# Self attention in a transformer block: another order of the projections between the heads, and x turned in two halves

## The reference, cut to what matters

```python
x_norm = modulate(_ln(x), shift_a, scale_a)
qkv = x_norm @ W_qkv + b_qkv
attn_w = softmax(einsum('bhqd,bhkd->bhqk', q, k) * scale)
attn_out = (attn_w @ v) @ W_proj + b_proj
x = x + gate_a[:, None] * attn_out
q_c = _ln(x) @ W_qc + b_qc
kv_c = _ln(context) @ W_kvc + b_kvc
...                                   # cross attention of q_c with k_c, v_c; x = x + its projection
h = gelu(modulate(_ln(x), shift_m, scale_m) @ W_mlp1 + b_mlp1) @ W_mlp2 + b_mlp2
x = x + gate_m[:, None] * h
```

## Time and profile before

| | us |
|---|---|
| median of three executions | 3124.63 |
| lowest, highest | 3118.6, 3124.9 |
| the profiled execution, its own time | 3114.64 |
| its span, first to last instruction | 3112.3 |
| TensorE busy in the span | 2748.2 (88%) |
| VectorE busy | 1821.6 (59%) |
| GpSimd busy | 1281.2 (41%) |
| ScalarE busy | 1091.0 (35%) |
| mean granted TensorE clock, share of full | 0.94 |

### The profile page before, as it was taken

How to read it: one execution, slowest core, us unless ns; L and a number is a source line. 1 busy time by engine, 2 the same in 40 slices (tenths; PEclk the granted TensorE clock), 3 DMA queues, 4 the chain that set the end, 5 groups by cost and what they waited for, 6 DMA issues and landing times. The chain is left out here.

```text
span 3112.3 us, 49898 instructions
## 1 busy us (share of the span) xinstructions
PE 2748.2 (88%) x18560; PEld 2183.8 (70%) x18560; DVE 1821.6 (59%) x3386; ACT 1091.0 (35%) x2083; POOL 1281.2 (41%) x1446
## 2 busy tenths in 40 slices
PE   3789989998972699999999999999955999999998
PEld 1667777777752577777777777777634888888886
DVE  2466766766653377777777777776635444444441
ACT  2234434433331144444444444444433211222110
POOL 1234333433330056666666666666761022202211
PEclk9889999999975999999999999999966999999999
DMA  5343434342412233333333333333413111111110
GB/s 167 84 114 82 125 82 126 83 126 79 123 57 88 73 97 105 104 104 104 104 104 104 104 104 104 104 106 83 105 59 112 34 38 48 45 35 39 46 45 21
DMA packets 170390, 269.79 MB, mean 87 GB/s; under 512 B 28967, under 2 KB 85287, under 8 KB 170135
## 3 DMA queue, kind: packets, MB, share of 16 engines
q1 hardware_dynamic: 167079, 259.26, 30.8%
q0 software_dynamic: 3072, 7.34, 0.7%
HBM read 111.04 MB, written 36.77 MB: 47 GB/s over the span
## 5 line engine op out<-in xcount | busy, mean ns | idle before, releaser
L1370 ACT ACTIVATE cross_prT<-cross_tr_ps 125x448 f32<-125x448 f32 x768 | 404.8, 543 | 359.8 <-PE cross_tr_ps L1168 347.6
L1268 DVE TENSOR_REDUCE cross_nmax<-cross_sc_ps 112x1 f32<-112x750 f32 x512 | 459.4, 929 | 37.6 <-PE cross_sc_ps L1151 37.2
L1415 POOL TENSOR_TENSOR cross_part<-cross_prT 125x448 f32<-125x448 f32 x256 | 293.2, 1145 | 339.9 <-PE cross_or_ps L1188 226.1
L860 POOL TENSOR_TENSOR self_psum<-self_prT 112x224 f32<-112x224 f32 x256 | 170.7, 667 | 471.5 <-PE self_or_ps L534 221.7
L1168 PE MATMUL cross_tr_ps<-cross_qst,cross_kst 98*125 98x224 f32 x1536 | 308.8, 286 | 26.8 <-DVE cross_cT_l L1251 22.3
L1168 PEld LDWEIGHTS cross_tr_ps<-cross_qst,cross_kst 98*125 98x125 f32 x1536 | 242.1, 188 | 101.6 <-issue 45.3
L1151 PE MATMUL cross_sc_ps<-cross_kst,cross_qst 96*112 96x500 f32 (+1 forms) x1024 | 280.7, 356 | 25.9 <-DVE cross_nmax L1268 11.6
L1417 POOL TENSOR_TENSOR cross_part<-cross_part,cross_prT 125x448 f32<-125x448 f32 x256 | 294.0, 1148 | 20.1
L1798 ACT ACTIVATE mlp_hv<-mlp_h_ps,mlp_b 128x512 f32<-128x512 f32 x112 | 77.2, 689 | 521.2 <-PE mlp_h_ps L70 507.3
L777 ACT ACTIVATE self_prT<-self_st_ps 112x448 f32<-112x448 f32 x256 | 139.0, 544 | 301.4 <-PE self_st_ps L514 301.4
L1725 DVE CAST mlp_hT_h<-mlp_hv 128x512 fp32r<-128x512 f32 x112 | 53.8, 481 | 321.7 <-ACT mlp_hv L1798 321.7
(11 more groups left out here) (175 smaller groups left out, 6769.6 us busy)
## 6 DMA issues: line engine op xcount, KB each, us to landing
cross_kst<-cross_nat_h SPq DMA_DIRECT2D x512, 93.8 KB, 2.2
cross_kst<-cross_nat_l SPq DMA_DIRECT2D x256, 93.8 KB, 2.2
cross_c_in<-in_context SPq DMA_DIRECT2D x90, 250.0 KB
cross_qst<-qc SPq DMA_DIRECT2D x192, 112.0 KB, 2.5
self_kst<-self_nat_h SPq DMA_DIRECT2D x128, 112.0 KB, 2.3
self_qst<-self_natq_h SPq DMA_DIRECT2D x128, 112.0 KB, 2.7
mlp_x<-in_w_mlp SPq DMA_DIRECT2D x32, 256.0 KB
self_x_in<-in_x SPq DMA_DIRECT2D x16, 448.0 KB, 6.9
```

Of the source, the lines that this page charges most:

```text
L860: pool.tensor_tensor(psum[:, j], prT[:, j, 0], prT[:, j, 1], ALU.add).then_inc(p_summed, 1)
L1268: dve.tensor_reduce(nmax[:, g % 2, t, j:j + 1], sc_ps[t][0:QN, SC0:SC0 + S], AX_X, ALU.max, negate=True).then_inc(maxed, 1)
L1370: act.activation(prT[:, slot(h), 2 * c:2 * c + 2], bank((h + LAG) % NH, c)[0:SN, 0:2 * N].rearrange("p (k t) -> p k t", k=2), ACT.Exp).the ...
L1415: pool.tensor_tensor(part[:], prT[:, j, 0:2], prT[:, j, 2:4], ALU.add).then_inc(pre_summed, 1)
```

## The change: what it does

1. **Order of the fills.** k moves from steps 2 to 4 to steps 0 to 3, one part a step. v moves from steps 13 to 15 and 0 to steps 7 to 9, still within the same body. c moves from steps 7 to 9 to steps 13 to 15, and its last part to step 0 of the body after; so the bodies run to b = 18. q, p, tx and ty stay, save that q's first part has step 4 with ty only.
2. **x in halves.** `high_x` and `low_x` work on two halves of the channels, and run in steps 13 and 14 (ScalarE) and 14 and 15 (GpSimd) of the body before, no more in step 0. k's first part waits for the first half, and after two of its four chunks for the second.
3. **c into `natq`.** The waits on the store of c and on the stacking move accordingly: q's first `highs` waits for the store of c, c's first `highs` for the stacking of q.
4. **SyncE.** `store_qc` moves to the head of the body, behind `load_x`; the second `place_maxima` moves ahead of `load_res`.

```diff
-        FILL = [[("v", 1, 1)], [], [("k", 0, 0)], [("k", 0, 1), ("k", 1, 0), ("ty", 0, 0)],
-                [("k", 1, 1), ("q", 0, 0), ("ty", 1, 0)], [("q", 0, 1), ("q", 1, 0)], [("q", 1, 1)], [("c", 0, 0)],
-                [("c", 0, 1), ("c", 1, 0)], [("c", 1, 1)], [("p", 0, 0)], [("p", 0, 1), ("p", 1, 0)],
-                [("p", 1, 1), ("tx", 0, 0)], [("v", 0, 0), ("tx", 1, 0)], [("v", 0, 1)], [("v", 1, 0)]]
+        FILL = [[("c", 1, 1), ("k", 0, 0)], [("k", 0, 1)], [("k", 1, 0)], [("k", 1, 1), ("ty", 0, 0)],
+                [("q", 0, 0), ("ty", 1, 0)], [("q", 0, 1), ("q", 1, 0)], [("q", 1, 1)], [("v", 0, 0)],
+                [("v", 0, 1), ("v", 1, 0)], [("v", 1, 1)], [("p", 0, 0)], [("p", 0, 1), ("p", 1, 0)],
+                [("p", 1, 1), ("tx", 0, 0)], [("c", 0, 0), ("tx", 1, 0)], [("c", 0, 1)], [("c", 1, 0)]]
...
-            for c in range(B + 2):
-                body(Batch(c), c < B, c < B - 1, 0 < c < B + 1, c > 1)
+            for c in range(B + 3):
+                body(Batch(c), c < B, c < B - 1, 0 < c < B + 1, 1 < c < B + 2)
...
                 if far(b):
                     load_x(b.plus(2))
+                if b.c > 2:
+                    store_qc(y3)
                 if att:
                     place_maxima(b, 0)
                 if nxt:
                     stack(a, k_l, nat, kst, k_stacked, (0, 1, 0))
+                if att:
+                    place_maxima(b, 1)
                 if prv:
                     load_res(z)
-                if att:
-                    place_maxima(b, 1)
                 if nxt:
                     stack(a, q_l, natq, qst, q_stacked, (0, 0, 1))
-                if old:
-                    store_qc(y2)
...
+                    if halves is not None and k % 2 == 0:
+                        pe.wait_ge(xT_l, halves.n(2, k // 2 + 1))
...
-                    pe.wait_ge(xT_l, o.n(1, 1))
-                    channels(c, part, wqkv, KC + 2 * c, xT, k_ps)
+                    channels(c, part, wqkv, KC + 2 * c, xT, k_ps, o if c == 0 and part == 0 else None)
...
-            def high_x(b):
-                act.wait_ge(xT_v, b.n(2, 2))
+            def high_x(b, c):
+                act.wait_ge(xT_v, b.n(2, c + 1))
                 wait(act, v_ps, b.n(2, 0))
-                act.copy(xT[0][:], xv[:]).then_inc(xT_h, 1)
+                act.copy(xT[0][:, 2 * c:2 * c + 2], xv[:, 2 * c:2 * c + 2]).then_inc(xT_h, 1)
...
-                        wait(act, qc_out, o.n(32, -96))
                     highs(o, c, k_ps, k_h, bqkv, KC + 2 * c, nat)
                 if kind == "q" and part == 1:
                     if c == 0 and o.c > 0:
                         act.wait_ge(q_stacked[1 - o.par], o.plus(-1).pair(STACK, STACK))
+                        wait(act, qc_out, o.n(32, -96))
...
-                        act.wait_ge(k_stacked[near % 2], Batch(near).pair(STACK, STACK))
+                        act.wait_ge(q_stacked[near % 2], Batch(near).pair(STACK, STACK))
                         wait(act, qc_out, o.n(32, 0))
-                    highs(o, c, c_ps, c_h, bqcs, 2 * c, nat)
+                    highs(o, c, c_ps, c_h, bqcs, 2 * c, natq)
...
-                    if nxt and h == 0:
-                        high_x(b.plus(1))
+                    if far(b) and h in (13, 14):
+                        high_x(b.plus(2), h - 13)
...
-                    if h == 0 and nxt:
+                    if h in (14, 15) and far(b):
                         after_sums(b, h)
-                        low_x(a)
-                        pool.wait_ge(xT_l, a.n(1, 1))
+                        low_x(far_b, h - 14)
```

More of the change, by code:

```diff
@@ L327, in self_phase @@
         block = ctx.enter_context(nc.Block())
-        FILL = [[("v", 1, 1)], [], [("k", 0, 0)], [("k", 0, 1), ("k", 1, 0), ("ty", 0, 0)],
[3 rows of a table removed]
+        FILL = [[("c", 1, 1), ("k", 0, 0)], [("k", 0, 1)], [("k", 1, 0)], [("k", 1, 1), ("ty", 0, 0)],
[3 rows of a table added]
         BANKS = [f for step in FILL for f in step if f[0][0] != "t" and f[2] == 0]
         def of(f):
-            return 0 if f == ("v", 1, 1) else {"k": 1, "q": 1, "v": 1, "p": -1, "c": -2, "tx": 2, "ty": -2}[f[0]]
+            return -3 if f == ("c", 1, 1) else {"k": 1, "q": 1, "v": 1, "p": -1, "c": -2, "tx": 2, "ty": -2}[f[0]]
         def exists(b, f):
@@ L419, in store_qc @@
                 for s in range(2):
-                    sp.dma_start(qc[b.c, s].rearrange("(g p) n -> p g n", p=P), nat[s][:].bitcast(F32)).then_inc(qc_out, 16)
+                    sp.dma_start(qc[b.c, s].rearrange("(g p) n -> p g n", p=P), natq[s][:].bitcast(F32)).then_inc(qc_out, 16)
             def body(b, att, nxt, prv, old):
-                a, z, y2 = b.plus(1), b.plus(-1), b.plus(-2)
+                a, z, y3 = b.plus(1), b.plus(-1), b.plus(-3)
                 if far(b):
                     load_x(b.plus(2))
+                if b.c > 2:
+                    store_qc(y3)
                 if att:
@@ L460, in trans, with channels @@
                 last.then_inc(done, 1)
-            def channels(c, m, w, first_chunk, src, done):
+            def channels(c, m, w, first_chunk, src, done, halves=None):
                 at = (first_chunk + m) * P
                 for k in range(KC):
+                    if halves is not None and k % 2 == 0:
+                        pe.wait_ge(xT_l, halves.n(2, k // 2 + 1))
                     last = product(pe, pj_ps[c][:, m * N:(m + 1) * N], (w[0][:, k, at:at + P], w[1][:, k, at:at + P]),
@@ L628, in modulate @@
                 if c == 0:
-                    wait(dve, xT_l, b.n(1, 0))
+                    wait(dve, xT_l, b.n(2, 0))
                 dve.wait_ge(xT_ps, b.n(2, c + 1))
@@ L691, in evict @@
                 if kind == "c" and part == 1:
-                    lows(o, c, c_h, c_l, bqcs, 2 * c, nat)
+                    lows(o, c, c_h, c_l, bqcs, 2 * c, natq)
                 if kind == "p" and part == 1:
@@ L833, in _ @@
                 apply_ln(a, t, x_in, x_in, rs1, nm1, nmr1, xhat1)
-            high_x(a)
+            for c in range(2):
+                high_x(a, c)
             start = Batch(-1)
@@ L840, in _ @@
                     apply_ln(a.plus(1), h - 9, x_in, x_in, rs1, nm1, nmr1, xhat1)
+                if h in (13, 14):
+                    high_x(a.plus(1), h - 13)
             bodies(body)
@@ L849, in rstd, with low_x @@
                 pool.tensor_tensor(rs[:], ve[:], neg_half[0:QN, 0:QT], ALU.pow).then_inc(s_rstd, 1)
-            def low_x(b):
-                pool.wait_ge(xT_h, b.n(1, 1))
-                pool.tensor_tensor(xT[1][:], xv[:], xT[0][:].bitcast(F32), ALU.subtract).then_inc(xT_l, 1)
+            def low_x(b, c):
+                at = slice(2 * c, 2 * c + 2)
+                pool.wait_ge(xT_h, b.n(2, c + 1))
+                pool.tensor_tensor(xT[1][:, at], xv[:, at], xT[0][:, at].bitcast(F32), ALU.subtract).then_inc(xT_l, 1)
+                pool.wait_ge(xT_l, b.n(2, c + 1))
             def sum_p(b, h):
@@ L899, in _ @@
             rstd(a, mv1, ve1, rs1, mvs1, vareps1, rstd1)
-            low_x(a)
-            pool.wait_ge(xT_l, 1)
+            for c in range(2):
+                low_x(a, c)
             pool.memset(ones[:], 1.0).then_inc(constant, 1)
@@ L907, in _ @@
             pool.wait_ge(rstd1, 2)
+            for c in range(2):
+                low_x(a.plus(1), c)
             bodies(body)
```

## The result

Four executions of the changed kernel have a median of 2992.43 us (2991.53 to 2995.88), those of the kernel before beside them 3123.99 us (3118.6 to 3124.9). The ratio is 0.9584, interval 0.9568 to 0.9601: 131.6 us less. Forecast were 3007 and a range of 2985 to 3045. The profiled execution took 2991.85 us, its span is 2990.1 us and its mean clock 0.957 (before: 3114.64, 3112.3, 0.940).

A forecast was written before the change was run, and what follows sets the result against it. TensorE bounds the kernel, idling once a batch for xT_l and the maxima, with lost clock. Gains of 125 us less 7 of small waits take 3114.6 to 2996.6; plus 10.0 gives a median of 3007, range 2985 to 3045.

The forecast's parts named there:

- start and two bodies, to batch 2: Before batch 2: 5 us from the start, 16.8 us from waits and clock in the two bodies.
- twelve batches: Self attention, 196.48 to 813.77 us: waits of 39.4 and 17.8 us and 37.0 of clock go, 94.2 us.
- small new waits: All 14 batches: 0.5 us a batch of new TensorE waits set against the gain, 7 us.
- 813.77 on, and the end: After the twelve batches: 4.4 us of waiting and clock, plus 5 us from c filling TensorE's final wait.
- profiled execution to median: Whole kernel: the median lies 10.0 us above the profiled execution, making 2996.6 us a median of 3007.
- One batch without its waits: Self attention batch: without waits and clock loss 43.6 us against 51.4, a floor for these instructions.
- both parts of the price: A TensorE wait costs its length and, when long, half the half-rate stretch behind it, 1.7 us in one case.
- The x chain: Batch turn: xT_l's second piece is ready 0.3 us before k's third chunk, removing 39.4 us of waits.
- The maxima: Second group's maxima: DMA leaves earlier in SyncE's queue, so their wait, 17.8 us in twelve batches, goes.
- the rival of late maxima: Maxima stay late or a like wait replaces theirs, about 35 us in all: 3042 us; chance 0.16.
- rival on VectorE: VectorE becomes the bound where bodies meet, 1 to 2 us a batch: about 3025 us; chance 0.09.
- the one on ScalarE for `natq`: ScalarE stands for c's stores and the q stack; a 10 us stop a batch gives 3147 us; chance 0.04.

The follow-up runs named there:

- e6: Changed kernel with one more GpSimd subtraction, into a spare tile, ahead of the second piece of xT_l; 3007.28 us, 0.9632.
- e7: Changed kernel with three more GpSimd subtractions, into a spare tile, ahead of the second piece of xT_l; 3068.55 us, 0.9826.
- e3: Changed kernel with x made in one piece, in steps 14 (ScalarE) and 15 (GpSimd); 3017.32 us, 0.9688.
- e4: Changed kernel with x made in one piece back in step 0, where it stood before; 3083.98 us, 0.9900.
- e1: Kernel before with only the second group's maxima moved ahead of x_res and the gate in SyncE's queue; 3082.03 us, 0.9901.
- e2: Changed kernel with x_res and the gate again ahead of the second group's maxima on SyncE; 3003.21 us, 0.9643.
- e9: Changed kernel with k back in steps 2 to 4 and x_res and the gate ahead of the second group's maxima; 3018.61 us, 0.9690.
- e11: Changed kernel run once more, unchanged; 2990.38 us, 0.9590.
- e5: Changed kernel with c written into nat again, its waits moved back with it; 3065.45 us, 0.9822.
- e12b: Kernel before, in its own order, with x for the next batch made in two pieces, both in step 0; 3095.51 us, 0.9926.

## Why the prediction was right, and where it was not

The trace has landmarks in both kernels: the first maxima row of batches 2 and 14 and the last `lows` of c. VectorE before, then after:

```profile
203.83 0.38 DVE L676 CAST self_mrow<-self_tx_ps 8x224 fp32r<-8x224 f32 x1 [2.67 <-PE self_tx_ps L502]
...
821.37 0.38 DVE L676 CAST self_mrow<-self_tx_ps 8x224 fp32r<-8x224 f32 x1 [2.92 <-PE self_tx_ps L502]
...
943.99 0.81 DVE L640 SCALAR_TENSOR_TENSOR self_nat_l<-self_pj_ps,self_bqcs,self_nat_h 128x224 fp32r<-128x224 f32 x2 [1.79 <-ACT self_nat_h L763]
```

```profile
190.54 0.38 DVE L677 CAST self_mrow<-self_tx_ps 8x224 fp32r<-8x224 f32 x1 [1.43 <-PE self_tx_ps L504]
...
712.31 0.38 DVE L677 CAST self_mrow<-self_tx_ps 8x224 fp32r<-8x224 f32 x1 [1.42 <-PE self_tx_ps L504]
...
821.43 0.81 DVE L641 SCALAR_TENSOR_TENSOR self_natq_l<-self_pj_ps,self_bqcs,self_natq_h 128x224 fp32r<-128x224 f32 x2 [1.78 <-ACT self_natq_h L764]
```

The lead is 13.3 us at batch 2, 109.1 at batch 14 and 122.6 at the end of the phase, at 822 us where about 825 were forecast; the cross attention and the MLP keep it (122.2 at the end of the span).

| step of the prediction | forecast | measured |
|---|---|---|
| start and two bodies, to batch 2 | 5 + 16.8 = 21.8 | 13.3 |
| twelve batches | 94.2 | 95.8 |
| small new waits | -7 | 0 |
| 813.77 on, and the end | 4.4 + 5 = 9.4 | 13.5 |
| sum, in profiled executions | 118 | 122.6 |
| profiled execution to median | +10.0 | +0.6 |

That the sum is off by 4.6 us only is in part luck: the start fell short by 8.5, and the 7 us set aside for small waits, which never came, and 4.1 more at the end made up for it. The twelve batches, four fifths of the gain, were forecast for the right reason.

- **One batch without its waits.** 43.6 us were worked out, 43.48 measured, every batch alike. Adding the waits and the time missing at 0.94 is what made this exact; e6, e7 and e3 bear out both parts of the price.
- **The x chain.** 0.3 us to spare forecast, 0.29 measured. e6 shows how thin: 1.2 us more on GpSimd is 0.8 us of waiting. e4 shows that the new order without this chain loses 92 of the 132 us and is no better than the exchange on SyncE alone (e1).
- **The maxima.** Gone, as taken. The 4.55 us from issue to use gave room for the 2.1 of an empty queue; e2 and e9 show that the rival of late maxima was near: without the exchange 0.6 us, without k's move too the whole wait.
- **VectorE.** Blocking by GpSimd of up to 2.2 us a batch was feared. The groups by line over twelve batches, before, then after (busy us, mean ns), show less time, not more:

```profile
L652 DVE SCALAR_TENSOR_TENSOR self_oT_l<-self_ou,self_bqkv,self_oT_h 128x224 fp32r<-128x224 f32 x48 | 26.4, 549 | 0.0
...
L625 DVE SCALAR_TENSOR_TENSOR self_nm<-self_mv,self_rs 112x2 f32<-112x2 f32 x24 | 21.4, 891 | 0.0
```

```profile
L653 DVE SCALAR_TENSOR_TENSOR self_oT_l<-self_ou,self_bqkv,self_oT_h 128x224 fp32r<-128x224 f32 x48 | 21.3, 444 | 0.0
...
L626 DVE SCALAR_TENSOR_TENSOR self_nm<-self_mv,self_rs 112x2 f32<-112x2 f32 x24 | 3.6, 151 | 0.0
```

  VectorE is busy 1.9 us a batch less there, (26.4 - 21.3 + 21.4 - 3.6) / 12, and 75 percent of the time, not 79. The `nm` operation (L626) meets no piece of xT_l any more. The `oT_l` operation (L653) still meets the first piece in each of the twelve batches, starts 0.02 us behind it and keeps its plain time; it is GpSimd's piece that takes 1.46 us where the second takes 1.15. VectorE, then GpSimd at 483.94:

```profile
483.96 0.45 DVE L653 SCALAR_TENSOR_TENSOR self_oT_l<-self_ou,self_bqkv,self_oT_h 128x224 fp32r<-128x224 f32 x1
```

  At the end of body 0 the same two meet 0.07 us apart, and there VectorE pays, 1.33 us for 0.44, until just after the piece is over:

```profile
130.44 1.33 DVE L653 SCALAR_TENSOR_TENSOR self_oT_l<-self_ou,self_bqkv,self_oT_h 128x224 fp32r<-128x224 f32 x1
```

```profile
130.37 1.15 POOL L858 TENSOR_TENSOR self_xT_l<-self_xv,self_xT_h 128x448 fp32r<-128x448 f32 x1
```

  The Trainium skill (SBUF — State Buffer, "Who interferes with whom") has the loser fully blocked. The trace agrees at 130.44; in the twelve batches the one that lost was GpSimd, and it lost 0.3 us only, less than the 0.45 of VectorE's operation. So the 7 us charged for small waits had nothing behind them here.
- **The start: the step that failed most.** In the table it is 8.5 us short. Some of that is the landmark: at the first maxima row of batch 2 the changed kernel has 24 matmuls more behind it, two parts of k (the counts of the first column, before, then after):

```profile
0.00:203.83 203.83, 130.93 (x816) 93.70 (x817) 87.10 (x180) 55.25 (x99) 44.45 (x57) 0.87 0.42 118
```

```profile
0.00:190.54 190.54, 132.63 (x840) 97.14 (x840) 87.74 (x182) 56.69 (x105) 45.18 (x61) 0.88 0.45 126
```

  TensorE starts its 817th matmul at 203.84 before and at 188.03 after: 15.8 us of lead, 6.0 less than the 21.8. The term that failed is the clock: it gave back 2.0 us where 6.2 were forecast. The granted clock is 0.84 over the 97.8 us from 106 us to the 817th matmul before, and 0.85 over the 91.0 us from 97 us to it after. Next, the waits for xT_l and the maxima did go, from 14.6 us to 2.9 between 75 us and that matmul, but others came: 3.0 us for the first stacks (0.6 before), and 4.7 us of the turns of x for VectorE (none before). With the smaller ones TensorE's idle time there fell by 12.4 us, from 25.5 to 13.1, where the prediction takes off 14.0. Against this, the first k of the kernel gave 2.9 us that it had nowhere: in halves, the wait of 4.1 us there is 1.3. TensorE after:

```profile
97.99 0.68 PE L486 MATMUL self_sc_ps<-self_kst,self_qst 96*112 96x224 f32 x2 [3.00 <-DMA self_qst<-self_natq_l]
...
127.12 0.60 PE L459 MATMUL self_tx_ps<-shared_ident,self_x_in 112*128 112x112 f32 x4 [2.20 <-DVE self_xv L634]
...
178.79 0.39 PE L68 MATMUL self_pj_ps<-self_xT_l,self_wqkv_h 128*128 128x224 f32 x1 [1.74 <-POOL self_xT_l L858]
```

  The first stacks, the second turn of x and, in body 1, again xT_l are late. The prediction knew that the fills are thin there and nothing covers the chain, and still put new waits at nothing.
- **The end.** The 7.69 us of the earlier trace rows became

```profile
808.18 0.98 PE L459 MATMUL self_tx_ps<-shared_ident,self_x_res 112*128 112x112 f32 x4 [3.59 <-ACT self_x_res L754]
```

  so c's part filled 4.1 of them, inside the forecast's 0 to 10 and near its 5. At the same matmul (the 5329th, at 821.38 and 709.80) the lead by batch 14 is 111.6 us, so 11.0 are left for the end, not 13.5, against 9.4 forecast. The forecast leaves out the wait of 3.78 us for the last maxima at 898.69, though the earlier trace rows show it; after, no wait for maxima is listed behind batch 14.
- **The median.** The prediction carried over the 10.0 us by which the median lay above the profiled execution. The profiled execution before was quicker than all four timed ones; that after lies 0.6 us below its median, and that of e11 5.1 above. These 9.4 us are most of the 14.6 between 3007 and 2992.4, and the profile showed no reason for either. The batches before are uneven, 49.9 to 53.8 us in one execution, and its executions spread from 3109 to 3129 us over these comparisons, on several chips. The new ones are all 43.48. Still e11's five executions spread over 8.9 us, not under 5 as expected, so uneven batches are not all of it. What the rest is stays open.

Neither rival on VectorE, nor the one on ScalarE for `natq`, showed: TensorE waits for nothing in the twelve batches. e5 shows what that stop would have looked like, in the other buffer.

## What to carry to other kernels

Where an engine is the bound and still waits once in every round, subtract from the round its waits and its time missing at the granted clock; if what hides the waits can be named, that floor is the forecast, and it held here to 0.3 percent. It holds where the rounds are alike; for the first rounds, where other waits lie close behind, it gave 6 us too much. A wait is worth shortening even if it can't be removed: between e7 and e6, 3.2 us cut to 0.8 gave back 4.4 us a round. When an order is moved, look for who then holds each buffer at its new place (v in step 0, `nat` in e5); and forecast the median against the median, not with one execution's distance to it.

## What was not expected of the hardware

- Behind idle stretches of 0.8 and 1.2 us the clock stayed at 1.00 (e6, e3), behind 2.3 us (e12b) TensorE ran at half rate for 6.4 us, from 497.93 on:

```profile
497.93:504.35 6.42, 6.42 (x38) 5.16 (x38) 1.33 (x4) 1.26 (x3) 1.32 (x2) 0.50 0.01 3
```

- It is not the length alone: e9 has maxima waits of up to 2.5 us and a clock of 0.99 from 200 to 700 us, where its batches vary from 44.9 to 48.4 us. What else decides is open.
- Two operations that meet on VectorE and GpSimd can cost either of them. VectorE's `oT_l` takes 0.87 us for 0.44 when it starts 0.06 us behind GpSimd's sum (549.27 and 549.21 before) and 1.33 when it starts 0.07 us behind a piece of xT_l (130.44 after), but keeps its 0.45 when it starts 0.02 us behind one (483.96), and GpSimd takes 0.3 us more instead. What decides is not shown.
- Two 128x448 pieces on GpSimd back to back (e12b) take 2.35 us, the whole 2.07: halving costs 0.3 us of GpSimd's time and still brought 24.5 us.
